# A fused attention and routing kernel: small reciprocals, five rotary operations, maxima spread over slots, ScalarE for scaling and max rows

## The reference, cut to what matters

```python
q, k = (_rope(q), _rope(k))        # y2[..., 0] * c - y2[..., 1] * s,  y2[..., 0] * s + y2[..., 1] * c
energy = jnp.einsum('bhtd,bhld->bhtl', q, k) + mask
attn = jax.nn.softmax(energy, axis=-1)
out = jnp.einsum('bhtl,bhld->bhtd', attn, v)
...
x = _layernorm(x + attention(x) @ wo.T)
ri = jnp.concatenate([xf, _stats(xf)], -1)      # mean, std, min, max, norm, share of near zeros
h = jax.nn.gelu(ri @ r1_w.T + r1_b)             # router, then top 2 of 32 experts, adapters, second layernorm
```

## Time and profile before

| | us |
|---|---|
| median of 3 runs | 2724.74 (2720.03 to 2725.88) |
| the profiled execution | 2717.94 |
| its span, first to last instruction | 2716.0 |
| TensorE busy in the span | 2082.1 |
| mean granted TensorE clock | 0.819 |

### The profile page before, as it was taken

One profiled execution on the slowest core, in us unless ns is written; L12 is line 12 of the kernel. 1 busy time (PEld: TensorE's weight loads), 2 busy tenths in 40 slices (PEclk: granted clock), 3 DMA queues, 4 the chain that ended last, 5 costly groups with the idle time before them and its releaser, 6 DMA issues. The chain is left out here.

```text
span 2716.0 us, 35735 instructions
## 1 busy us (share of the span) xinstructions
PE 2082.1 (77%) x10274; PEld 1451.5 (53%) x10274; DVE 1749.5 (64%) x3464; ACT 1068.7 (39%) x2549; POOL 1414.2 (52%) x2003
## 2 busy tenths in 40 slices
PE   4787888788878788888787888775422799999990
PEld 3454444444544444444444544442422799999990
DVE  7554675686567568567657756764568656656564
ACT  2133233333323323323333332332242666666665
POOL 2377376447546636745744752332101666677653
PEclk7698797888878879878877987776555899999995
DMA  1000011000001001100100100110300144454437
GB/s 58 4 17 14 8 32 32 28 30 30 18 14 39 30 20 32 34 8 26 36 24 28 36 20 3 34 39 32 122 0 0 38 153 138 146 167 142 156 81 248
DMA packets 100605, 143.71 MB, mean 53 GB/s; under 512 B 17956, under 2 KB 88592, under 8 KB 96364
## 3 DMA queue, kind: packets, MB, share of 16 engines
q1 hardware_dynamic: 84588, 131.78, 14.2%
q0 software_dynamic: 15872, 10.24, 2.3%
HBM read 112.87 MB, written 39.85 MB: 56 GB/s over the span
## 5 line engine op out<-in xcount | busy, mean ns | idle before, releaser
L611 ACT ACTIVATE probs<-scores_t_ps 128x512 f32<-128x512 f32 (+3 forms) x640 | 338.8, 534 | 817.6 <-PE scores_t_ps L496 423.7
L713 DVE TENSOR_REDUCE part_max<-scores_ps 128x1 f32<-128x512 f32 (+3 forms) x640 | 377.3, 605 | 107.3 <-PE scores_ps L476 48.1
L476 PE MATMUL scores_ps<-k_st,q_two 128*128 128x512 f32 (+3 forms) x640 | 337.6, 552 | 123.7 <-DVE part_max L713 87.2
L869 POOL TENSOR_TENSOR products<-qk,cos_sin 128x128 f32<-128x128 f32 x464 | 216.0, 495 | 286.1 <-ACT qk L586 262.5
L325 POOL TENSOR_TENSOR sums<-sums,probs 128x512 f32<-128x512 f32 (+3 forms) x288 | 325.4, 1130 | 28.4 <-ACT probs L611 27.1
L512 PE MATMUL out_ps<-probs,v_sb 128*64 128x512 f32 (+3 forms) x1280 | 328.7, 642 | 0.0
L495 PE MATMUL scores_t_ps<-q_two,k_st 128*128 128x512 f32 (+3 forms) x640 | 298.3, 466 | 2.5 <-ACT probs L611 2.2
L1479 PE MATMUL up_ps<-xe_t,w 128*128 128x320 f32 x1920 | 288.9, 310 | 2.4 <-DVE xe_t L1586 1.7
L1479 PEld LDWEIGHTS up_ps<-xe_t,w 128*128 128x128 f32 x1920 | 283.6, 189 | 3.0 <-issue 1.9
L476 PEld LDWEIGHTS scores_ps<-k_st,q_two 128*128 128x128 f32 x640 | 150.5, 237 | 237.2 <-DVE part_max L713 182.9
L325 DVE TENSOR_TENSOR sums<-sums,probs 128x512 f32<-128x512 f32 (+3 forms) x288 | 238.6, 829 | 38.1 <-ACT probs L611 31.1
(11 more groups left out here) (251 smaller groups left out, 3790.9 us busy)
## 6 DMA issues: line engine op xcount, KB each, us to landing
w_raw<-in_w_expert SPq DMA_DIRECT2D x32, 1536.0 KB, 6.5
x_t<-in_x_t SPq DMA_DIRECT2D x128, 128.0 KB, 2.0
w_raw<-in_w_adapter SPq DMA_DIRECT2D x32, 384.0 KB, 7.4
x_row<-in_x SPq DMA_DIRECT2D x64, 128.0 KB, 2.0
x_rows<-x SPq DMA_DIRECT2D x64, 128.0 KB, 2.0
acc_rows<-x SPq DMA_DIRECT2D x64, 128.0 KB, 2.0
ln_x<-acc_rows SPq DMA_DIRECT2D x16, 512.0 KB, 6.1
out_rows_dram<-ln_y SPq DMA_DIRECT2D x16, 512.0 KB, 5.2
```

Source lines behind the costliest of these rows:

```text
L476: mm = pe.matmul(out[:, 0:n], q_two[:, ring, hh, cols(i)], k_st[:, h, c * CH:c * CH + n], start=True, stop=not diagonal)
L611: act.activation(probs[:, g % P_RING, i * P:CH], s_ps[:, g % 2, i * P:CH], ACT.Exp).then_inc(exp_done, 1)
L713: dve.tensor_reduce(part_max[:, u % 4, i, c:c + 1], x_ps[:, e % 2, 0:n], AX.X, ALU.max).then_inc(score_read, 1)
L869: last = eng.tensor_tensor(products[:, a], x, cos_sin[:, table, t, :].unsqueeze(1).to_broadcast([P, 4, HD // 2]), ALU.mult)
```

## The change

- **Reciprocals.** `sum` uses eight matmuls with a selecting matrix, so that the sums of 2 heads x 4 tiles lie on 8 partitions x 128 columns; VectorE takes their reciprocal in a new step `sum_read`. A new late step `spread`, a slot or more later, spreads them over 128 x 512 by four matmuls, ScalarE copies that into `attn` and VectorE multiplies.
- **Rotary.** The weights' rows are put in halves (even, odd) on the host and a table of negated sines is added: three products and two sums in place of four and four.
- **Plan.** At most two maxima entries a slot up to six slots before the group begins; projections at other slots; x_t three slots ahead, `sum` one slot later, statistics and x1's transposes one and two slots later. 4 query places for 3, 8 places of exponentials for 6.
- **24 places** for keys and values of one pair of heads, in a ring over all phases, in place of 16 tiles x 4 heads.
- **ScalarE** copies the max rows (L710 before) and scales x1 (L772 before) as y * rstd + shift, where the shift, minus mean times rstd, comes from one more small operation each of VectorE and GpSimd. x_row gets two places.

```diff
-P_RING = 6
+P_RING = 8
 BATCH = 4
-Q_RING = 3
+Q_RING = 4
+KEEP = 24
 ROW_RING = 12
...
-            base_of[n] = base = 3 * (n - FIRST) if f == 0 else 12 + 4 * t if f == 1 else per * (f - 1) + 5 * t
+            if f == 0:
+                base = 3 * (n - FIRST)
+            elif t < 8:
+                base = per * (f - 1) + (14 + 5 * t if f == 1 else 8 + 6 * t)
+            else:
+                base = per * (f - 1) + 54 + 4 * (t - 8)
+            base_of[n] = base
...
+        sum_at, spread_at = [], []
         for y in range(len(self.groups)):
-            at = begin[y + 1]
-            while ("a", at) in used:
-                at += 1
-            used.add(("a", at))
-            sum_at.append(at)
+            sum_at.append(free("a", begin[y + 1] + 1))
+            spread_at.append(free("a", sum_at[y] + 1))
...
-                at = max(at + pace if post else 0, sum_at[y] + 1)
...
+        for y in range(len(self.groups)):
+            late[sum_at[y]].append(("sum", y))
+            early[sum_at[y] + 1].append(("sum_read", y))
+            late[spread_at[y]].append(("spread", y))
+            early[spread_at[y] + 1].append(("norm", y))
...
-                late[max(base - 2, 0)].append(("xt", n))
+                late[max(base - 3, 0)].append(("xt", n))
             late[base].append(("proj", n))
             early[base + 1].append(("proj_read", n))
             late[base + 6].append(("kt", n))
             early[base + 7].append(("kt_read", n))
             turned[n] = base + 7
...
-        q_from, self.q_bank = [], {n: "ab"[n % 2] for n in range(8)}
-        for y, (f, G) in enumerate(self.groups):
-            at = begin[y] - 2 * self.size[2 * y] - 10
-            if y >= Q_RING:
-                at = max(at, begin[y - Q_RING + 1] - 1)
-            elif y == 2:
-                at = 0
...
+        for y, (f, G) in enumerate(self.groups):
+            at = min(s for s, u, _, _ in entries if u // 2 == y) - 10
+            if y >= Q_RING:
+                at = max(at, begin[y - Q_RING + 1] - 1)
+            elif y >= 2:
+                at = max(at, 0)
+            for i in range(4):
+                n = f * NT + 4 * G + i
+                if y >= 2:
+                    at = max(at, base_of.get(n, -10) + 5)
+                    while ("a", at) in used and ("b", at) in used:
...
+            q_from.append(at + 2)
...
             f = self.groups[y][0]
+            s = max(wanted, at)
             if u >= 4:
                 s = max(s, q_from[y])
-            s = max(s, turned.get(f * NT + 4 * c + 3, -100) + 1, at)
+            s = max(s, turned.get(f * NT + 4 * c + 3, -100) + 1)
+            while s >= 0 and s < begin[y] - 6 and taken.get(s, 0) >= 2:
+                s += 1
+            taken[s] = taken.get(s, 0) + 1
...
-            late[at + 4].append(("stats", m))
-            late[at + 6].append(("x1t", m))
-            early[at + 7].append(("x1t_read", m))
-            late[at + 7].append(("hidden", m))
-            early[at + 8].append(("hidden_read", m))
+            late[at + 5].append(("stats", m))
+            late[at + 8].append(("x1t", m))
+            early[at + 9].append(("x1t_read", m))
+            late[at + 9].append(("hidden", m))
+            early[at + 10].append(("hidden_read", m))
...
-        h = projection(n)[1]
-        return slice(h, h + 2)
+    def place(n):
+        return n % KEEP
+
+    def places(n, count=1):
+        return slice(n % KEEP * P, (n % KEEP + count) * P)
+
+    def before_place(n):
+
+        f, t = divmod(n - KEEP, NT)
+        return begin[NG * f + NG - 1] + 2 * t + 2 if n >= KEEP else 0
...
-                at_least(sp, resid_done, m)
-                sp.dma_start(x_row[:], dram["x"][m * P:(m + 1) * P, :]).then_inc(xrow_loaded, 16)
+                at_least(sp, resid_done, m - 1)
+                sp.dma_start(x_row[:, m % 2, :], dram["x"][m * P:(m + 1) * P, :]).then_inc(xrow_loaded[m % 2], 16)
...
                 elif kind == "sum":
                     claim("a", totals_read, k + 1)
+                    if k == 0:
+                        pe.wait_ge(masks_set, 5)
                     for hh in range(2):
                         pe.wait_ge(summed[hh], begin[k + 1] // 2)
-                        mm = pe.matmul(a_ps[hh * HD:(hh + 1) * HD, :], ones[:], sums[:, k % 2, hh, :],
+                        for i in range(4):
+                            n = 4 * hh + i
+                            mm = pe.matmul(a_ps[0:8, 0:P], pick[:, n, :], sums[:, k % 2, hh, cols(i)],
+                                           start=n == 0, stop=n == 7)
+                    mm.then_inc(totals_ready, 1)
+                elif kind == "spread":
+                    claim("a", spread_copied, k + 1)
+                    pe.wait_ge(totals_read, k + 1)
+                    for i in range(4):
+                        mm = pe.matmul(a_ps[:, cols(i)], spread[0:8, i].rearrange("p a b -> p (a b)"), inverse[:],
                                        start=True, stop=True)
-                    mm.then_inc(totals_ready, 1)
+                    mm.then_inc(spread_done, 1)
...
+                if n >= KEEP:
+                    act.wait_ge(values_done, (before_place(n) - 1) // BATCH + 1)
+                act.copy(v_sb[:, place(n)], ps[:, QK:QKV].rearrange("p (h d) -> p h d", h=2))\
...
+                at_least(act, scores_ready, before_place(n))
+                act.copy(k_st[:, :, places(n)], ps.rearrange("p (h d) -> p h d", h=2)).then_inc(k_upper, 1)
...
+                u, c, _ = plan.entries[e]
+                if c is None:
+                    _, _, hh, ring = unit(u)
+                    act.wait_ge(scored, e + 1)
+                    if u // 2 >= Q_RING:
+                        act.wait_ge(scores_ready, begin[u // 2 - Q_RING + 1])
+                    act.copy(q_low[HD:HD + 1, ring, hh, :], x_ps[HD:HD + 1, e % 2, :]).then_inc(row_read, 1)
 
             def main(g):
+                for e in plan.score_at[g]:
+                    score(e)
                 if g + S_AHEAD < CHUNKS:
                     exp(g + S_AHEAD)
...
+                elif kind == "norm":
+                    f, G = groups[k]
+                    act.wait_ge(spread_done, k + 1)
+                    act.wait_ge(weights_split, 8)
+                    at_least(act, attn_split, NT * (f // 2 - 1) + 4 * G + 4)
+                    act.copy(attn[:, f % 2, G * CH:(G + 1) * CH], a_ps[:]).then_inc(spread_copied, 1)
...
+                elif kind == "x1":
+
+                    act.wait_ge(shift_ready, k + 1)
+                    if k >= 2:
+                        act.wait_ge(x1_stored[k % 2], 32 * (k // 2))
+                        act.wait_ge(x1_turned, k - 1)
+                    act.activation(x1[:, k % 2, 0:D], y[:], ACT.Identity, scale=rstd[:], bias=shift[:])\
+                       .then_inc(x1_ready, 1)
...
+                if c is None:
+                    return
                 dve.wait_ge(scored, e + 1)
-                if c is None:
-                    dve.tensor_copy(q_low[HD:HD + 1, ring, hh, :], x_ps[HD:HD + 1, e % 2, :]).then_inc(score_read, 1)
-                    return
                 n = (i + 1) * P if c == G else CH
...
+                    if u >= 2:
+                        dve.wait_ge(scored, plan.row_entry[u - 2] + 1)
...
                 elif kind == "norm":
                     f, G = groups[k]
-                    dve.wait_ge(totals_ready, k + 1)
-                    at_least(dve, attn_upper, NT * (f // 2 - 1) + 4 * G + 4)
+                    dve.wait_ge(spread_copied, k + 1)
+                    dve.wait_ge(values_done, begin[k + 1] // BATCH)
                     out = attn[:, f % 2, G * CH:(G + 1) * CH]
-                    dve.reciprocal(out, a_ps[:]).then_inc(totals_read, 1)
-                    dve.drain()
-
-                    dve.wait_ge(values_done, begin[k + 1] // BATCH)
                     dve.tensor_tensor(out, o_ps[:, r, :], out, ALU.mult).then_inc(attn_ready, 1)
                     dve.drain()
+                elif kind == "sum_read":
+                    dve.wait_ge(totals_ready, k + 1)
+                    dve.reciprocal(inverse[:], a_ps[0:8, 0:P]).then_inc(totals_read, 1)
...
-                    dve.tensor_tensor(y[:], b_ps[:, 0:D], x_row[:], ALU.add).then_inc(resid_done, 1)
+                    dve.wait_ge(xrow_loaded[r], 16 * (k // 2 + 1))
+                    at_least(dve, x1_ready, k)
+                    dve.tensor_tensor(y[:], b_ps[:, 0:D], x_row[:, r, :], ALU.add).then_inc(resid_done, 1)
...
-                    dve.tensor_scalar(mean_var[:, 2:3], mean_var[:, 1:2], LN_EPS, None, ALU.add).then_inc(var_ready, 1)
-                elif kind == "x1":
-
-                    dve.wait_ge(rstd_ready, k + 1)
-
-                    if k >= 2:
-                        dve.wait_ge(x1_stored[r], 32 * (k // 2))
-                        dve.wait_ge(x1_turned, k - 1)
-                    dve.tensor_scalar(x1[:, r, 0:D], y[:], mean_var[:, 0:1], rstd[:], ALU.subtract, ALU.mult)\
```

(48 more changed lines are left out.)

110 lines of the change are left out of this document (56 added, 54 removed).

## The result

The changed kernel takes 2459.5 us against 2725.3 us, a ratio of 0.903 (95% interval 0.901 to 0.905). That is inside the range I gave, 2450 to 2700, at its lower edge, and 109 us under my 2569. The case I named for it, "the clock rises more", had 0.10.

The account below looks back on a forecast made before the run. No engine is full; TensorE's idle time plus work / clock bounds attention: idle 274 + 1359 (1223 at 0.90) = 1633 against 1780, -147, and -9 at the end: 2562, median 2569 us. Range 2450 to 2700, its own 2490 to 2650.

Parts of the forecast that it names:

- the clock rises more: Rival for attention's stretch: clock 0.94 and idle 215 us, since a faster TensorE stutters less; about 2452 us; chance 0.10.
- since their other gaps stay: Reason for taking clock 0.90, that of stretches without bursts, in attention: 1223 us of full-clock work becomes 1359.
- Bursts make the clock low: In attention, 17 maxima at one slot go with clock 0.58; at most three a slot with 0.90 and 0.93.
- ScalarE's new wait for the shift: Scaling x1, ScalarE waits for GpSimd's power and second operation, exponentials queued behind: +20 us idle (64 x 0.3).
- the sign of being right: TensorE's waits for VectorE's maxima (L713), 87.2 us before, were to come under 25 us.
- Work: TensorE's full-clock work in attention: 24 short matmul instructions a group, 2.64 us against 1.0, +52 us in all.
- The collision: Key turn and next projection share a slot and PSUM bank, 50 slots against three: 47 x 1.5 = +70 us idle.
- The slower rival: Collisions in attention take 3.6 us each, 169 us, and keep the clock at 0.82: about 2800 us; chance 0.10.
- at nothing of their own: Cost given to the fourth query place and eight probability places, which let maxima entries come earlier.
- maxima spread: Never more than three maxima entries a slot: of TensorE's 87.2 us waiting for maxima 20 stay, -67 us.
- Reciprocal: At a group's end, 0.84 us instead of 3.36; 40.4 us of waits go, 13 put back for handovers: -27 us idle.
- The end: After the last sum, order wo, next wo, x1 lets two rows overlap: about 3 us off three turns, -9.

Follow-up runs that it names:

- the old slots: Changed kernel with a row tile's statistics, transposes and hidden layer at slots 4, 6 and 7 after, not 5, 8 and 9: 2539.8 us, ratio 0.932.
- four kernels: Changed kernel, 2460 us; it without the maxima limit, 2488; with 3 query places, 2547; with no limit and 3 query places, 2562.

## Why the prediction was right, and where its sizes were off

The frame held: a stretch is idle time + work / clock, and the three terms moved the way I forecast. Two of them were mis-sized, both in the same direction: I forecast 156 us less and 266 were measured. 2459.5 us lies outside the forecast's own range, 2490 to 2650; the stated range holds it only because it took in the rival "the clock rises more", whose clock of 0.94 came and whose idle time of 215 us became 240. That is luck as far as the 2569 goes.

- **The clock, 58 us too little.** I took 0.90 "since their other gaps stay", from stretches that were smooth before. But those still had gaps for x_t (2.9 us of the 19.0 idle in 568 to 668 us), the reciprocal (2.1) and the statistics (1.9), which other parts of the same change took away, and it became 0.94: 1223 / 0.90 - 1223 / 0.94 = 58 us. This is the step that failed. "Bursts make the clock low" was also only a part of it: the kernel before without its bursts got 0.85, and the changed kernel with three query places has no burst and yet 0.90. The runs show that nearly every undone part moves the clock as well as the idle time: the query place is 63 us of busy time and 28 of idle time, the old slots 41 and 32. A gap should have been priced at more than its own length.
- **Idle time, 37 us too little.** I forecast -78 and measured -115. Statistics went to 1.0 instead of 20 us, x_t to 0.7 instead of 22, the last sum's wait for GpSimd from 18.7 to 0. ScalarE's new wait for the shift, +20 in my sum, hardly reached TensorE: its waits for exponentials (L530) are 5.9 us where they were 1.7. The other way: L713's successor kept 46 us where I kept 20 and had named 25 as the sign of being right, and a new wait came for attn_t (21.7), which I hadn't seen. The waits for the queries' subtraction (27.2 at L458) aren't new: before they stood at several lines, 28.5 us in all.
- **Work, +44 against +52.** The 24 instructions took 2.94 us, not 2.64, so by themselves +62 a kernel, and undoing them took 66 away; the clock's two digits (0.5% is 7 us) don't allow more than to say that the term was of the right size. The trace agrees with the packing rule of the Trainium skill (TensorE: Matmul & The Clock Gate, Part 3): instructions on one group of columns followed each other, 16 of 128 columns in 1.85 us, 0.90 ns a column, where the four of 512 columns of the old sum, on both halves, took 1.01 us, 0.49 ns a column. The 81 ns for 128 columns of the Trainium skill (the same page, Back-to-back issue gap) were less than the 116 that they took (1.85 / 16).
- **The collision, right.** 53 waits of 1.67 us where I had 50 of 1.5; keeping one slot between them gave 82 us, though that run moves queries too. The slower rival had its place right, and neither its price (3.6 us each) nor its clock (0.82).
- **The query and exponential places, "at nothing of their own": wrong and right.** The fourth query place is worth 87 us, the largest part measured, the two of exponentials nothing. The work of the "maxima spread" is thus the earlier queries, with the other slots and banks that they take, rather than the limit (28 us).
- **Reciprocal.** 0.94 us (I had 0.84); undone it costs 73 us. By my own terms the part was a loss, -27 idle and 52 / 0.90 = +58 busy; it paid because 88 us of idle time hung on it, not 27, and because the clock fell to 0.90 without it.
- **Scaling on ScalarE.** I took 60 us off VectorE for it, booked no gain in time and put 20 us against it; the run gives 0 (3 us, within what I don't read). The quoted rule of the Trainium skill (ScalarE: Activation LUTs, Rules for kernel authors), by which the move gains nothing, comes out right for this operation, though not for the reason: 0.60 us on ScalarE is under the 0.93 on VectorE. My 0.415 for ScalarE was too low. That the wait for the shift takes the gain back is likely, but no run shows it by itself. For the max rows the same move gained 22 us.
- **The end.** In the last rows x1's turns stood 9.4 us apart; the stretch behind the last group is 6.8 us shorter, I had 9. After, TensorE in order of time:

```profile
1619.29 0.66 PE L603 MATMUL misc_ps<-ident,x 128*128 128x128 f32 x2 [0.94 <-POOL x L933]
...
1625.51 0.66 PE L603 MATMUL misc_ps<-ident,x 128*128 128x128 f32 x2 [0.95 <-POOL x L933]
...
1633.94 0.69 PE L603 MATMUL misc_ps<-ident,x 128*128 128x128 f32 x2 [0.52 <-DVE y L828]
1640.25 0.66 PE L603 MATMUL misc_ps<-ident,x 128*128 128x128 f32 x2 [5.40 <-POOL x L933]
```

The three steps are 6.2, 8.4 and 6.3 us, the overlap that I had argued from the order.

The single parts, undone one at a time, come to 87 + 80 + 73 + 28 + 22 + 15 + 3 = 308 us, and the collision takes 82 back: 226 against the 266 measured. They aren't independent (the limit costs 28 us with four query places and 15 with three), so the sum is only a check of size. Not tried alone: the 24 places for keys and values, x_t one slot earlier, the sum one slot later, the new spacing of the projections apart from the collision, and the second place of x_row.

## What to carry to other kernels

Price the tensor engine's stretch as idle time + work / clock, and a gap at more than its length: where this kernel lost a gap, between a quarter and all of what it won was the clock. When a plan moves operations to other slots, look for pairs that newly share a bank in one slot; here one slot between them was worth 82 us. And look at how evenly the work lies over the slots, not only at how much of it there is: with three query places the work was the same and the kernel 87 us slower.

## What the runs showed of the hardware that I hadn't expected

- The same instructions (6696 or 6697 records) were busy for 1307, 1331, 1370 and 1388 us in four kernels, at granted clocks of 0.94, 0.92, 0.90 and 0.89.
- ScalarE's scaling of 128 x 256 with a column each for scale and bias took 0.60 us, its square of as many elements 0.415.
- The reciprocal of 128 columns on 8 partitions took 0.946 us, of 512 columns on 128 partitions 3.358: (3.358 - 0.946) / 384 = 6.3 ns a column and about 0.14 us besides, an estimate from two shapes that differ in partitions too.
